# Another order of the steps in the period of the long attentions

## The chip, the cores and the metric

The kernel runs on one core of one Trainium2 chip. The metric is the time of one execution on the device, in microseconds (us); less is better. The engines are TensorE (PE; its weight loads are PEld), VectorE (DVE), ScalarE (ACT), GpSimd (POOL) and SyncE (SP), each with its own in-order program, tied by semaphores.

## The reference, cut to what matters

```python
# L0, L2 and L3 each hold one attention of 448 tokens (8 batches x 56) over a context of 1500 positions per batch
q = heads(norm(x) @ Wq + bq)                    # 16 heads of 8 features
k, v = heads(norm(context) @ Wkv + bkv)         # L0 modulates norm(context); L3 uses the context as it is
attn = softmax(q @ k.T / sqrt(8))
x = x + (attn @ v) @ Wp + bp
```

Between them stand a single-head attention over the same context and three experts (L1), self-attentions over the 56 tokens, and MLPs. The change touches the three long attentions alone.

## The kernel before

A `Heads` object emits one long attention. Its unit is a **period**: the work around the scores of one batch n. TensorE, ScalarE, VectorE and GpSimd each have a list of step names (`self.orders`, built in `Heads.__init__`), and `run` emits them in that order. A step works for batch n, n+1 or n+2 (its lead), so that a period holds:

- for n: `S0`..`S11`, the scores of a chunk of 125 keys each (8 products into one of two score buffers, line 568); on ScalarE `E0`..`E11`, their exponential (line 660); `PV0`..`PV5`, probabilities times values of two chunks (24 products, line 580). `S` of chunk c waits for `E` of c-2, `PVk` for `E(2k+1)`.
- for n-1: `OT`, `OTT`, turning and normalising its output (lines 598 to 609; VectorE lines 706 to 725).
- for n+1: `M0.0`..`M2.7`, 24 products of 128x500 scores each (line 554), of which VectorE takes the maximum (line 687); then VectorE's `maxall`, `maxb`, `part0`, `part1` (lines 690 to 699), TensorE's `MTa`, `MTb` (line 544), which turn the maxima, and `shift0` (VectorE, line 703) and `shift1` (ScalarE, line 664), which copy them into two rows of the queries. `S0` of the next period waits for both.
- for n+2: `T0`..`T2`, transposes of the normalised context (line 523, only where `hat` is set, the first two attentions; ScalarE line 624), `K0`..`K2`, key projections (line 531; each read by two copies on ScalarE, `k0.j` and `Kj`, line 642; GpSimd then splits the rest and SP's DMAs stack the parts, line 365), and `V0`..`V2`, value projections (line 538; two copies on ScalarE, lines 648 and 649).

`T`, `K`, `V`, `M`, `MT`, `OT` and `OTT` write one of three PSUM banks of a ring, `ring_ps`. `ring_banks` hands them out in TensorE's order (the bank of `K1` and `K2` is passed over for a while), and a step waits until the reader of the bank's last user is done. VectorE's list follows TensorE's. ScalarE's is written out in the old kernel: `V0`, `V1`, `shift1`, `V2` come after `E11`.

The old order on TensorE with T steps, with its banks:

```
S0 M0.0:0 M0.1:1 S1 OT:2 T0:0 T1:1 T2:2 M0.2:0 S2 OTT:1 PV0 K0:2 S3 M0.3:0 M0.4:1 S4 K1:2 M0.5:0 PV1 M0.6:1
S5 M0.7:0 M1.0:1 M1.1:2 S6 M1.2:0 PV2 M1.3:1 S7 K2:2 M1.4:0 M1.5:1 S8 M1.6:0 M1.7:1 PV3 M2.0:2 S9 M2.1:0 M2.2:1
S10 M2.3:2 M2.4:0 PV4 M2.5:1 S11 M2.6:2 M2.7:0 V0:1 PV5 V1:2 MTa:0 MTb:1 V2:2
```

`later_periods` runs a fill (maxima of batch 0, its own list `fill`), a period for batch 0, four periods (batches 1 to 4) in a loop with register addresses, and batches 5, 6 and 7 straight; in batch 6's period nothing is left to do for n+2, in batch 7's nothing for n+1.

Of the kernel before, what the change touches and what calls it, by code (L numbers as in the profile page):

```python
# [25 lines left out]
NPV = NC // 2  # L26
# [179 lines left out]
def pixart_program(nc, ctx_nat, ctx_T, x_T, cond_T, weights, vectors, identity, out):  # L206
    ctx = ExitStack()
    with ctx:
# [6 lines left out]
        def sem(name):  # L215
            return ctx.enter_context(nc.semaphore(name))
# [158 lines left out]
        class Heads:  # L375
            def __init__(self, tag, wkey, wval, bkey, bval, hat, modulated=False):
                self.tag, self.wkey, self.wval, self.bkey, self.bval = tag, wkey, wval, bkey, bval
                self.hat, self.modulated = hat, modulated
                J = range(NJ)
                mm = [f"M{j}.{p}" for j in J for p in range(PAIRS)]  # L380
                self.mm = mm
                T3 = [f"T{j}" for j in J] if hat else []

                if hat:
                    beside = {0: mm[0:2], 1: ["OT", *T3, mm[2]], 2: ["OTT", "K0"], 3: mm[3:5], 4: ["K1", *mm[5:7]],
                              5: mm[7:10], 6: mm[10:12], 7: ["K2", *mm[12:14]], 8: mm[14:17], 9: mm[17:19],
                              10: mm[19:22], 11: mm[22:24]}
                else:
                    beside = {0: mm[0:1], 1: ["K0", "OT", mm[1]], 2: ["OTT", mm[2]], 3: ["K1", *mm[3:5]], 4: mm[5:7],
                              5: ["K2", *mm[7:9]], 6: mm[9:12], 7: mm[12:14], 8: mm[14:17], 9: mm[17:19],  # L390
                              10: mm[19:22], 11: mm[22:24]}
                pe = []
                for c in range(NC):

                    more = beside.get(c, [])
                    pe += [f"S{c}", *more[:-1]] + ([f"PV{c // 2 - 1}"] if c and c % 2 == 0 else []) + more[-1:]
                pe += ["V0", f"PV{NPV - 1}", "V1", "MTa", "MTb", "V2"]

                act = []
                for c in range(NC):  # L400
                    act += [f"E{c}", *(T3 if c == 1 else [])]
                    for j in J:
                        if f"K{j}" in beside.get(c, []):
                            act += [f"k0.{j}", f"K{j}"]
                act += ["V0", "V1", "shift1", "V2"]
                read = {"OT": ["sum0", "sum1", "norm0", "norm1"], "OTT": ["OTT"], **{m: [m] for m in mm}}
                dve = ["O", *[r for n in pe for r in read.get(n, [])], "maxall", "maxb", "part0", "part1", "shift0"]
                pool = (["deps", "dpow", "norm", "hat0", "hat1", "hat2"] if hat else []) + [f"{s}{j}" for j in J for s in ("rest", "k1.", "k2.")]
                LEAD = {"S": 0, "P": 0, "E": 0, "O": -1, "s": -1, "n": -1, "T": 2, "K": 2, "V": 2, "k": 2, "h": 2, "r": 2, "d": 2}

                def lead(n):
                    return 2 if n == "norm" else 1 if n in ("shift0", "shift1") else LEAD.get(n[0], 1)

                self.lead = lead
                if modulated:
                    fill = [*mm[0:8], "T0", *mm[8:10], "T1", *mm[10:12], "T2", "K0", *mm[12:16], "K1", *mm[16:20], "K2",
                            *mm[20:24], "V0", "V1", "MTa", "MTb", "V2"]
                else:
                    fill = [*T3, "K0", "K1", "K2", "V0", "V1", *mm, "MTa", "MTb", "V2"]
                self.fill = fill  # L420
                self.orders = {"pe": pe, "act": act, "dve": dve, "pool": pool}

                of_context = {"pe": "TKV", "act": "TkKV", "dve": (), "pool": "dnhrk"}

                def context(eng, n):
                    mine = of_context[eng]
                    return n in mine if isinstance(mine, tuple) else n[0] in mine

                self.context = context
                self.plans = {}  # L430
                for eng, order in self.orders.items():
                    for which in (False, True):
                        steps = [(n, lead(n)) for n in order if context(eng, n) == which]
                        kind = "context" if which else "attention"
                        self.plans[eng, which] = Periods(sem(f"{tag}_{eng}_{kind}_done"), steps) if steps else None
                self.loaded = [sem(f"{tag}_contextT_loaded{u}") for u in range(2)] if not hat else None
                self.nat_loaded = [sem(f"{tag}_context_loaded{u}") for u in range(2)] if hat else None
                self.stacked = [[sem(f"{tag}_keys_stacked{u}_columns{j}") for j in J] for u in range(2)]
                self.qstacked = sem(f"{tag}_queries_stacked")
                self.rows_clear = sem(f"{tag}_rows_clear")  # L440

                self.reader = {}
                for j in J:
                    self.reader |= {f"T{j}": ("act", f"T{j}"), f"K{j}": ("act", f"K{j}"), f"V{j}": ("act", f"V{j}")}
                for m in mm:
                    self.reader[m] = ("dve", m)
                self.reader |= {"MTa": ("dve", "shift0"), "MTb": ("act", "shift1"), "OT": ("dve", "norm1"),
                                "OTT": ("dve", "OTT")}
# [1391 lines left out]
```

How the kernel before makes its waits and increments, by code:

```python
def wait_steps(eng, n, *steps):  # L171
    last = {}
    for plan, name, d in steps:
        last[plan] = max(last.get(plan, -9999), plan.place(name, d))
    for plan, at in last.items():
        eng.wait_ge(plan.sem, n * len(plan.names) + at)
# [336 lines left out]
                def emit(name, batch, prev, cur, nxt):  # L514
# [3 lines left out]
                    if name[0] == "T":  # L518
                        wait_steps(pe, n, self.at("pool", f"hat{name[1:]}"), *free)
                        j = int(name[1:])
                        for c in range(CJ):
                            last = pe.transpose(ps[:, c * CK:(c + 1) * CK], hat_sb[:, j * CJ + c, :],
                                                ident[0:CK, 0:CK])
                    elif name[0] == "K":
                        j = int(name[1:])
                        if self.loaded and j == 0:
                            pe.wait_ge(self.loaded[u], 16 * (half + 1))
                        wait_steps(pe, n, *([self.at("act", f"T{j}")] if self.hat else []), *free)
                        last = pe.matmul(ps[:, 0:KB], self.wkey, self.context_T(u)[:, j * KB:(j + 1) * KB],
# [15 lines left out]
                        j, p = (int(t) for t in name[1:].split("."))  # L547
                        if p == 0:
                            pe.wait_ge(self.stacked[u][j], REPLICA * (half + 1))
                        if name == self.mm[0]:
                            pe.wait_ge(self.qstacked, REPLICA)
                            pe.wait_ge(self.rows_clear, 1)
```

## Time and profile before

| | us |
|---|---|
| median of 3 runs | 1091.48 (1089.87 to 1096.06) |
| profiled execution | 1089.86 |
| its span | 1088.0 |
| TensorE busy | 956.8 (88%) |
| VectorE busy | 583.2 (54%) |
| ScalarE busy | 516.7 (47%) |
| GpSimd busy | 364.6 (34%) |

The long attentions take some 225 us each: about 45 to 285 us, 510 to 733 and 845 to 1058 of the span. Busy time of TensorE is modelled from the start of a product to the end of its result, so it says less than the distance from one step's start to the next. A bracket behind a row of the timeline is idle time of that engine just before it and what ended it.

### The profile page before, as it was taken

Reading aid. Unit: us, or ns where it says so; the run is one execution under the profiler, and the core shown is the slowest. Engines: PE = TensorE matmul, PEld = TensorE weight load, DVE = VectorE, ACT = ScalarE, POOL = GpSimd, SP = SyncE. Lnnn points to the kernel's source line nnn. Section 1 sums busy time; section 2 is a strip of 40 time slices with the busy share of each in tenths; the row PEclk is TensorE's granted clock in tenths of the full one; section 3 lists DMA queues with packets and bytes.
Section 4 is the critical chain, followed back from the end, with each engine's and each line's share of the span. In section 5 each row is a group of like instructions: output and inputs, shape, how many; then the busy total and the mean of one; then the engine's idle time right before and its main releaser. Section 6 shows DMA issues by size and latency. Waiting matters only on the chain.

```text
span 1088.0 us, 25068 instructions
## 1 busy us (share of the span) xinstructions
PE 956.8 (88%) x9448; PEld 619.3 (57%) x9448; DVE 583.2 (54%) x1281; ACT 516.7 (47%) x766; POOL 364.6 (34%) x489
## 2 busy tenths in 40 slices
PE   5659999998889988897899999978798899999977
PEld 3436666666556644583466666653385466666653
DVE  7575666666122166213666666735412666666735
ACT  5636666665223222313366666551222266666541
POOL 6565555540000003315555556110301333333100
PEclk9679999999989999658799999999867699999999
DMA  9753443437025311404344443200230644443200
GB/s 249 174 142 89 111 111 105 109 91 244 1 86 169 98 44 43 135 24 120 97 111 114 110 113 90 69 33 26 77 87 21 172 116 115 120 122 100 58 2 9
DMA packets 76823, 106.25 MB, mean 98 GB/s; under 512 B 9370, under 2 KB 70426, under 8 KB 76480
## 3 DMA queue, kind: packets, MB, share of 16 engines
q1 hardware_dynamic: 75152, 102.26, 34.0%
q10 hardware_dynamic: 1584, 2.79, 0.9%
q8 instruction: 60, 0.98, 0.4%
q14 instruction: 27, 0.22, 0.1%
HBM read 41.17 MB, written 0.23 MB: 38 GB/s over the span
## 4 chain that ended last, share of the span: by engine, by line
PE 64%; DVE 15%; issue 10%; ACT 6%; POOL 2%; DMA 1%; SPq 0%; ACTq 0%; POOLq 0%; DVEq 0%
PE oacc_ps L580 10%; PE ring_ps L554 10%; PE score_ps L568 7%; DVE max_sb L687 7%; PE ring_ps L538 6%; PE ring_ps L531 6%; PE oacc_ps L896 4%; PE ring_ps L1165 3%; PE oacc_ps L335 3%; PE ring_ps L1043 2%; PE score_ps L1035 2%; PE ring_ps L544 2%; PE ring_ps L523 2%; ACT key_sb L642 1%; PE ring_ps L1026 1%
## 5 line engine op out<-in xcount | busy, mean ns | idle before, releaser
L687 DVE TENSOR_REDUCE max_sb<-ring_ps 128x1 f32<-128x500 f32 x576 | 356.4, 673 | 174.2 <-PE ring_ps L554 174.1
L660 ACT ACTIVATE prob_sb<-score_ps 125x896 f32<-125x896 f32 x288 | 257.3, 919 | 132.5 <-PE score_ps L568 131.8
L554 PE MATMUL ring_ps<-kstack,qstack 128*128 128x500 bf16 x576 | 203.8, 392 | 25.0 <-DVE max_sb L687 17.1
L765 POOL TENSOR_TENSOR key_sb<-key_sb,part_sb 128x500 f32<-128x500 f32 x72 | 82.0, 1139 | 280.1 <-ACT key_sb L642 280.1
L568 PEld LDWEIGHTS score_ps<-qstack,kstack 128*128 128x128 bf16 (+1 forms) x2304 | 145.4, 102 | 48.4 <-issue 7.6
L568 PE MATMUL score_ps<-qstack,kstack 128*128 128x112 bf16 (+3 forms) x2304 | 167.4, 214 | 2.4 <-ACT qstack L664 2.3
L580 PE MATMUL oacc_ps<-prob_sb,val_sb 125*32 125x168 f32 (+1 forms) x3456 | 139.5, 294 | 12.7 <-ACT prob_sb L660 12.3
L580 PEld LDWEIGHTS oacc_ps<-prob_sb,val_sb 125*32 125x32 f32 x3456 | 97.7, 109 | 51.7 <-ACT prob_sb L660 23.6
L554 PEld LDWEIGHTS ring_ps<-kstack,qstack 128*128 128x128 bf16 (+1 forms) x576 | 52.5, 98 | 111.2 <-issue 59.7
L335 PE MATMUL oacc_ps<-ident,mean_mat 128*128 128x512 bf16 x326 | 90.3, 417 | 0.0
L756 POOL TENSOR_SCALAR hat_sb<-nat_sb,norm_now 125x128 f32<-125x128 f32 x192 | 87.7, 480 | 4.9 <-POOL norm_now L746 4.9
L772 POOL TENSOR_TENSOR part_sb<-key_sb,part_sb 128x500 bf16<-128x500 f32 x72 | 81.7, 1135 | 5.8
L1209 POOL TENSOR_TENSOR tok_rstd<-tok_var,minus_half 112x4 f32<-112x4 f32 x8 | 8.1, 1010 | 211.5 <-DVE tok_var L1223 211.5
L531 PE MATMUL ring_ps<-ctxT_sb,w_sb 128*128 128x500 f32 x96 | 58.8, 701 | 11.2 <-ACT key_sb L642 8.5
L642 ACT ACTIVATE part_sb<-ring_ps,vec_sb 128x500 bf16<-128x500 f32 x72 | 49.1, 682 | 33.5 <-PE ring_ps L531 31.0
L648 ACT COPY val_sb<-ring_ps 125x384 f32<-125x384 f32 x72 | 34.6, 481 | 56.2 <-PE ring_ps L538 56.2
L335 PEld LDWEIGHTS oacc_ps<-ident,mean_mat 128*128 128x128 bf16 x326 | 33.1, 107 | 44.5 <-issue 21.9
L538 PE MATMUL ring_ps<-w_sb,ctxT_sb 128*125 128x128 f32 x384 | 55.7, 292 | 1.8 <-ACT val_sb L649 1.5
L1243 ACT COPY qpart_sb<-prob_sb 64x448 bf16<-64x448 bf16 x30 | 16.9, 562 | 83.1 <-DVE prob_sb L1232 82.3
L1165 PE MATMUL ring_ps<-tok,w_sb 128*128 128x448 f32 x102 | 46.3, 587 | 10.2 <-DVE part_sb L1797 3.6
L538 PEld LDWEIGHTS ring_ps<-w_sb,ctxT_sb 128*125 128x125 f32 x384 | 47.9, 196 | 11.8 <-DVE max_sb L687 4.6
L523 PE MATMUL ring_ps<-ident,hat_sb 125*128 125x125 f32 x192 | 29.0, 300 | 23.8 <-DVE max_sb L687 9.0
(207 smaller groups left out, 1084.6 us busy)
## 6 DMA issues: line engine op xcount, KB each, us to landing
kstack<-part_sb SPq DMA_DIRECT2D x432, 125.0 KB, 2.4
nat_sb<-ctx_nat SPq DMA_DIRECT2D x24, 672.0 KB
nat_sb<-ctx_T SPq DMA_DIRECT2D x8, 750.0 KB, 4.3
qstack<-qpart_sb SPq DMA_DIRECT2D x24, 224.0 KB, 3.6
w_sb<-ctx_nat SPq DMA_DIRECT2D x5, 672.0 KB
w_sb<-weights SPq DMA_DIRECT2D x1, 3076.5 KB, 12.4
ctxT_sb<-ctx_T SPq DMA_DIRECT2D x4, 750.0 KB, 6.3
part_sb<-ctx_T SPq DMA_DIRECT2D x4, 750.0 KB, 5.9
```

The costliest lines, as they stand in the source:

```text
L335: pe.matmul(out.rearrange("p (a k) -> p a k", a=2), busy_lhs, busy_rhs, start=True, stop=True)
L531: last = pe.matmul(ps[:, 0:KB], self.wkey, self.context_T(u)[:, j * KB:(j + 1) * KB], start=True, stop=True)
L538: last = pe.matmul(ps[0:CK, c * D:(c + 1) * D], self.context_T(u)[:, k0:k0 + CK], self.wval, start=True, stop=True)
L554: last = pe.matmul(ps[:, 0:KB], queries(p, n, D), kstack[:, u, p, j * KB:(j + 1) * KB], start=True, stop=True)
L568: last = pe.matmul(score_ps[0:window(c), c % 2, p // 4, at:at + 2 * LQ], kstack[:, u, p, c * CK:c * CK + window(c)], queries(p, n), start= ...
L580: return pe.matmul(oacc_ps[tile * GW:(tile + 1) * GW, at:at + nh * LQ], val_sb[0:CK, u, c, g * GW:(g + 1) * GW], prob_sb[0:CK, c % PROBS, ...
L660: ins = act.activation(dst, score_ps[0:CK, c % 2, :, 0:HALF], ACT.Exp)
L687: ins = dve.tensor_reduce(max_sb[:, p, j:j + 1], ring_ps[:, self.bank[name], 0:KB], AX.X, ALU.max)
L756: ins = pool.tensor_scalar(hat_sb[:, c, :], nat_sb[0:CK, u, c, :], norm_now[:, 1, c:c + 1], norm_now[:, 0, c:c + 1], ALU.add, ALU.mult)
L765: ins = pool.tensor_tensor(rest, rest, part_sb[:, 0, cols], ALU.subtract)
L772: ins = pool.tensor_tensor(part_sb[:, 2, cols], rest, part_sb[:, 1, cols], ALU.subtract)
L1165: last = pe.matmul(self.ps(name) if out is None else out, lhsT, rhs, start=(k == 0), stop=(k == len(pairs) - 1))
```

## The change

TensorE's list is written out in slots: steps ahead of a chunk's scores, the scores, steps beside them. Two M steps now come ahead of `S0`; the others stand one or two at a time between the rest; `V0` and `V1` stand among the scores (ahead of `S9` and behind `S10` with T steps, ahead of `S8` and `S10` without); `T0`, `T1`, `T2` are apart from each other; `V2` comes ahead of `MTa`. `PVk` comes right behind `S(2k+2)`, and one M stands between `S11` and `PV5` instead of two and `V0`. ScalarE's list is drawn from TensorE's, so its copies of T, K and V stand among the exponentials where their products do. The fill lists put `V2` ahead of `MTa`.

```diff
                 if hat:
-                    beside = {0: mm[0:2], 1: ["OT", *T3, mm[2]], 2: ["OTT", "K0"], 3: mm[3:5], 4: ["K1", *mm[5:7]],
-                              5: mm[7:10], 6: mm[10:12], 7: ["K2", *mm[12:14]], 8: mm[14:17], 9: mm[17:19],
-                              10: mm[19:22], 11: mm[22:24]}
+                    slots = [([], "S0", mm[2:4]), (["OT", mm[4], "T0"], "S1", [mm[5]]), (["OTT", "T1"], "S2", ["PV0", mm[6]]),
+                             (["T2", mm[7]], "S3", [mm[8]]), (["K0"], "S4", ["PV1", *mm[9:11]]), ([mm[11]], "S5", ["K1", mm[12]]),
+                             ([], "S6", ["PV2", *mm[13:15]]), (["K2"], "S7", mm[15:17]), ([], "S8", ["PV3", *mm[17:19]]),
+                             (["V0"], "S9", mm[19:21]), ([], "S10", ["PV4", "V1", *mm[21:23]]), ([], "S11", [mm[23]])]
                 else:
-                    beside = {0: mm[0:1], 1: ["K0", "OT", mm[1]], 2: ["OTT", mm[2]], 3: ["K1", *mm[3:5]], 4: mm[5:7],
-                              5: ["K2", *mm[7:9]], 6: mm[9:12], 7: mm[12:14], 8: mm[14:17], 9: mm[17:19],
-                              10: mm[19:22], 11: mm[22:24]}
-                pe = []
-                for c in range(NC):
-
-                    more = beside.get(c, [])
-                    pe += [f"S{c}", *more[:-1]] + ([f"PV{c // 2 - 1}"] if c and c % 2 == 0 else []) + more[-1:]
-                pe += ["V0", f"PV{NPV - 1}", "V1", "MTa", "MTb", "V2"]
-
-                act = []
-                for c in range(NC):
-                    act += [f"E{c}", *(T3 if c == 1 else [])]
-                    for j in J:
-                        if f"K{j}" in beside.get(c, []):
-                            act += [f"k0.{j}", f"K{j}"]
-                act += ["V0", "V1", "shift1", "V2"]
+                    slots = [([], "S0", mm[2:4]), (["OT", mm[4]], "S1", [mm[5]]), (["OTT", "K0"], "S2", ["PV0", mm[6]]),
+                             ([mm[7]], "S3", [mm[8]]), (["K1"], "S4", ["PV1", *mm[9:11]]), ([mm[11]], "S5", [mm[12]]),
+                             (["K2"], "S6", ["PV2", mm[13]]), ([mm[14]], "S7", mm[15:17]), (["V0"], "S8", ["PV3", *mm[17:19]]),
+                             ([mm[19]], "S9", [mm[20]]), (["V1"], "S10", ["PV4", mm[21]]), ([mm[22]], "S11", [mm[23]])]
+                pe = [*mm[0:2]]
+                for ahead, scores, beside in slots:
+                    pe += [*ahead, scores, *beside]
+                pe += [f"PV{NPV - 1}", "V2", "MTa", "MTb"]
...
+                at_act = {"T": lambda n: [n], "K": lambda n: [f"k0.{n[1:]}", n], "S": lambda n: [f"E{n[1:]}"], "V": lambda n: [n]}
+                act = [step for n in pe if n[0] in at_act for step in at_act[n[0]](n)] + ["shift1"]
```

The new orders, with the banks that `ring_banks` gives:

```
with T:    M0.0:0 M0.1:1 S0 M0.2:2 M0.3:0 OT:1 M0.4:2 T0:0 S1 M0.5:1 OTT:2 T1:0 S2 PV0 M0.6:1 T2:2 M0.7:0 S3 M1.0:1
           K0:2 S4 PV1 M1.1:0 M1.2:1 M1.3:2 S5 K1:0 M1.4:1 S6 PV2 M1.5:2 M1.6:1 K2:2 S7 M1.7:0 M2.0:1 S8 PV3 M2.1:0
           M2.2:1 V0:2 S9 M2.3:0 M2.4:1 S10 PV4 V1:2 M2.5:0 M2.6:1 S11 M2.7:2 PV5 V2:0 MTa:1 MTb:2
without T: M0.0:0 M0.1:1 S0 M0.2:2 M0.3:0 OT:1 M0.4:2 S1 M0.5:0 OTT:1 K0:2 S2 PV0 M0.6:0 M0.7:1 S3 M1.0:2 K1:0 S4
           PV1 M1.1:1 M1.2:2 M1.3:1 S5 M1.4:2 K2:0 S6 PV2 M1.5:1 M1.6:2 S7 M1.7:1 M2.0:2 V0:0 S8 PV3 M2.1:1 M2.2:2
           M2.3:0 S9 M2.4:1 V1:2 S10 PV4 M2.5:0 M2.6:1 S11 M2.7:2 PV5 V2:0 MTa:1 MTb:2
ScalarE, with T: E0 T0 E1 T1 E2 T2 E3 k0.0 K0 E4 E5 k0.1 K1 E6 k0.2 K2 E7 E8 V0 E9 E10 V1 E11 V2 shift1
```

## Rows read from the trace of the kernel before

**Rows 1.** The page: busy time by engine, and the chain that ended last.
```profile
PE 956.8 (88%) x9448; PEld 619.3 (57%) x9448; DVE 583.2 (54%) x1281; ACT 516.7 (47%) x766; POOL 364.6 (34%) x489
...
PE 64%; DVE 15%; issue 10%; ACT 6%; POOL 2%; DMA 1%; SPq 0%; ACTq 0%; POOLq 0%; DVEq 0%
```

**Rows 2.** Windows cut at `part0`: stretch, length, busy us (instructions), clock, DMA.
```profile
104.73:216.93 112.20, 106.89 (x1304) 72.47 (x1294) 70.41 (x140) 74.72 (x114) 65.93 (x98) 1.00 0.41 111
216.93:243.40 26.47, 25.64 (x322) 17.35 (x318) 17.56 (x36) 18.26 (x28) 13.40 (x19) 1.00 0.33 88
243.40:265.90 22.50, 21.00 (x312) 14.34 (x301) 17.07 (x36) 12.59 (x19) 0.00 (x0) 1.00 0.94 304
555.08:665.70 110.62, 106.56 (x1304) 72.30 (x1293) 70.39 (x141) 72.94 (x114) 65.91 (x98) 1.00 0.42 113
...
887.46:992.28 104.82, 100.34 (x1248) 66.96 (x1242) 69.23 (x140) 67.05 (x102) 34.59 (x36) 1.00 0.42 118
992.28:1017.34 25.06, 24.32 (x318) 16.30 (x312) 17.15 (x36) 16.39 (x27) 8.65 (x9) 1.00 0.35 94
```

**Rows 3.** Timeline of TensorE, straight-line period: start, length, step.
```profile
218.00 1.04 PE L544 MATMUL ring_ps<-ident,maxparts 128*2 128x128 f32 x8
218.90 1.14 PE L538 MATMUL ring_ps<-w_sb,ctxT_sb 128*125 128x128 f32 x8
219.91 0.55 PE L568 MATMUL score_ps<-qstack,kstack 128*128 128x112 bf16 x8
...
226.24 0.56 PE L568 MATMUL score_ps<-qstack,kstack 128*128 128x112 bf16 x8
226.63 0.58 PE L554 MATMUL ring_ps<-kstack,qstack 128*128 128x500 bf16 x2
227.06 0.56 PE L568 MATMUL score_ps<-qstack,kstack 128*128 128x112 bf16 x8
...
242.82 0.97 PE L580 MATMUL oacc_ps<-prob_sb,val_sb 125*32 125x168 f32 x24
243.72 1.14 PE L538 MATMUL ring_ps<-w_sb,ctxT_sb 128*125 128x128 f32 x8
```

**Rows 4.** Timeline, end of the period without context steps (batch 6).
```profile
263.31 0.62 PE L568 MATMUL score_ps<-qstack,kstack 128*125 128x112 bf16 x8
...
263.97 0.92 ACT L660 ACTIVATE prob_sb<-score_ps 125x896 f32<-125x896 f32 x1 [1.30 <-PE score_ps L568]
264.94 0.73 PEld L580 LDWEIGHTS oacc_ps<-prob_sb,val_sb 125*32 125x32 f32 x24 [1.07 <-ACT prob_sb L660]
264.94 0.97 PE L580 MATMUL oacc_ps<-prob_sb,val_sb 125*32 125x168 f32 x24 [0.58 <-ACT prob_sb L660]
...
268.01 0.95 PE L568 MATMUL score_ps<-qstack,kstack 128*128 128x112 bf16 x16 [0.78 <-ACT qstack L664]
```

**Rows 5.** Timeline around `K2` of a loop period.
```profile
207.07 1.06 PE L531 MATMUL ring_ps<-ctxT_sb,w_sb 128*128 128x500 f32 x2
...
207.97 0.58 PE L554 MATMUL ring_ps<-kstack,qstack 128*128 128x500 bf16 x2
...
208.18 0.68 ACT L642 ACTIVATE part_sb<-ring_ps,vec_sb 128x500 bf16<-128x500 f32 x1
...
209.31 0.92 ACT L660 ACTIVATE prob_sb<-score_ps 125x896 f32<-125x896 f32 x1
```

**Rows 6.** Timeline of VectorE and ScalarE: eight maxima in a row, `V0`'s first copy.
```profile
238.04 4.91 DVE L687 TENSOR_REDUCE max_sb<-ring_ps 128x1 f32<-128x500 f32 x8 [0.52 <-PE ring_ps L554]
...
242.93 0.48 ACT L648 COPY val_sb<-ring_ps 125x384 f32<-125x384 f32 x1 [0.54 <-PE ring_ps L538]
```

**Rows 7.** Timeline of TensorE: `S0` of a loop period.
```profile
192.07 1.02 PE L568 MATMUL score_ps<-qstack,kstack 128*128 x8
```

**Rows 8.** Windows, columns as in Rows 2: end of stage two's fill, batch 7's period.
```profile
524.00:531.00 7.00, 5.07 (x18) 2.52 (x18) 4.75 (x12) 0.52 (x1) 3.41 (x8) 0.50 0.26 86
266.00:285.00 19.00, 13.98 (x260) 10.53 (x261) 2.44 (x10) 10.88 (x13) 0.00 (x0) 1.00 0.02 5
```

More of the change, by code:

```diff
@@ new lines, in __init__ @@
+                pe = [*mm[0:2]]
+                for ahead, scores, beside in slots:
+                    pe += [*ahead, scores, *beside]
+                pe += [f"PV{NPV - 1}", "V2", "MTa", "MTb"]
+                assert sorted(n for n in pe if n[0] == "M" and n[1] != "T") == sorted(mm)
+                at_act = {"T": lambda n: [n], "K": lambda n: [f"k0.{n[1:]}", n], "S": lambda n: [f"E{n[1:]}"], "V": lambda n: [n]}
+                act = [step for n in pe if n[0] in at_act for step in at_act[n[0]](n)] + ["shift1"]
@@ L416, in __init__ @@
                     fill = [*mm[0:8], "T0", *mm[8:10], "T1", *mm[10:12], "T2", "K0", *mm[12:16], "K1", *mm[16:20], "K2",
-                            *mm[20:24], "V0", "V1", "MTa", "MTb", "V2"]
+                            *mm[20:24], "V0", "V1", "V2", "MTa", "MTb"]
                 else:
-                    fill = [*T3, "K0", "K1", "K2", "V0", "V1", *mm, "MTa", "MTb", "V2"]
+                    fill = [*T3, "K0", "K1", "K2", "V0", "V1", *mm, "V2", "MTa", "MTb"]
                 self.fill = fill
```

## The prediction, made before the changed kernel was run

> **What bounds the kernel now.** I read the page first: TensorE is busy 88% of the span and 64% of the chain that ended last, VectorE 15%, ScalarE 6% [rows 1]. So TensorE's program order sets the time, and a step put elsewhere costs what TensorE then waits. Next the stage windows: a steady period of a long attention (one batch) takes 112.20 / 4 = 28.05 us in the first stage, 110.62 / 4 = 27.66 in the second, 104.82 / 4 = 26.21 in the third (no T steps); those are the four periods in the program's loop. The straight-line period behind them takes 26.47 and 25.06 us, and the one that has no context steps left 22.50 [rows 2]. The clock is at its upper level in all. The timeline then gives the price of each step, and what can be late.
>
> **Unit prices**, as the distance to the next step on TensorE: S 0.39 us, M (43 / 2) 0.21, PV 0.90, V 1.0, MTa and MTb together 0.90 [rows 3], K 0.90 [rows 5] (its reader starts 1.11 after it starts, so a result is seen about 0.2 after its stream ends). T (0.44), OT (0.78) and OTT (0.25) I take from the same stretch; they don't change. Sum of a period with T steps: 12 x 0.39 + 24 x 0.21 + 6 x 0.90 + 3 x 1.0 + 3 x 0.92 + 3 x 0.44 + 0.90 + 0.78 + 0.25 = about 24.2 us; without T 22.9. The straight-line periods leave 26.47 - 24.2 = 2.2 us of waits, and 25.06 - 22.9 = 2.1. Placing the old order step by step with these prices (a step starts when its engine is free and its releaser is done) gives 26.1 and 25.0 us, with waits of 1.9 and 2.1, nearly all of them M steps waiting for a ring bank whose maximum VectorE has not read; so I trust the method to about 0.4 us a period. VectorE starts a maximum each (4.91 - 0.68) / 7 = 0.60 us [rows 6], TensorE can issue one in 0.21; between stretches of maxima VectorE idles.
>
> **The change, part by part.** No instruction is added or removed: the 24.2 us of TensorE work stand, and so do the work of ScalarE and VectorE. Only waits change. I place the new order in the same way.
>
> (a) M steps spread out, two ahead of S0. This removes the old bank waits at M1.0, M1.6, M1.7, M2.4 and V0 (about 1.4 us in my placement). But with three banks, new neighbours meet: K2 now takes the bank of M1.5 with only M1.6 between. M1.5 starts, VectorE 0.41 later, its maximum takes 0.68: K2 can start at 1.14, TensorE arrives at 0.42, a wait of 0.72. OT waits for the maximum of M0.1 (0.39), T0 for M0.3 (0.22), OTT (0.20), K0 (0.21, behind T2's copy), K1 (0.11), small ones 0.1. Sum 1.95. In the stage without T: M1.3 0.72, M1.7 0.33, M2.0 0.39, V1 0.39, OT 0.39, K0 0.40, OTT 0.21, two of 0.11: 3.05.
>
> (b) PV5 follows S11 with one M between. The nearest row is the period without context steps: S11 starts at 263.31, its exponential at 263.97, PV5 at 264.94, which is 1.63 after S11, with 0.58 us idle although two M stand between [rows 4]. In a full period before, V0 fills this gap. After the change S11 (0.45) and one M (0.21) fill 0.66 of 1.6: a wait of 0.93 in every period. I take 0.93; the ends are 0.58 (the row) and 1.0.
>
> (c) ScalarE's order. Its list now follows TensorE's, so the two copies of K2 (0.57 each, 1.13 from the first copy to the exponential behind [rows 5]) stand right ahead of E7, and V0's two copies (the first takes 0.48 [rows 6]; both, queued, I estimate at 0.64) ahead of E9. E7 starts 0.2 + 1.15 after K2's stream ends, which is when S7 starts, and ends at 2.27; TensorE has S7, two M and S8 (1.21) and then stands at PV3, which needs E7: a wait of 1.1. In the same way PV4 waits for E9: 0.2 + 0.63 + 0.92 against 1.21, that is 0.54 to 0.6. Before, K2's copies came behind E7 and two more exponentials' worth of TensorE work lay ahead of PV3; V0 and V1 came after the last exponential. Behind PV3 on TensorE stand M2.1, M2.2, V0 and all that follows, so VectorE starves too. In the stage without T, K2 stands ahead of S6 and V0 ahead of S8, with no odd E right behind, and neither wait appears. Below, each could be zero if TensorE came late enough anyway; I keep that for the range.
>
> (d) V2 moves ahead of MTa. Before, V2 (1.0 us) ran while the two shift rows were copied into the queries; S0 followed at once (218.00, 218.90, 219.91 [rows 3]). Where no V2 stands there, S0 stands idle for 0.78 us [rows 4]. Now M0.0 and M0.1 (0.42) stand there, M0.1 itself in the bank of MTa and so behind its copy: 0.35 to 0.5 us of waiting per period. In exchange V2 covers the chain from the last maximum to the maxparts, but that chain was covered before by V0, PV5 and V1: no gain in a full period. S0 behind these two M asks for nothing else new: the keys' columns that M0.0 reads were stacked a period ago (DMA issues lie near the middle of a period), so SP's queue adds nothing; its waits on S3, S7, S11 keep their place. POOL works 65.93 / 4 = 16.5 us of 28 [rows 2] and has slack of over 1 us at T0.
>
> Sums of a straight-line period: with T 1.95 + 0.93 + 1.1 + 0.57 + 0.35 = 4.9 us of waits for 1.9, **+3.0**; without T 3.05 + 0.93 + 0.4 = 4.4 for 2.1, **+2.3 to +2.8**. The period without context steps: +1.4 and +1.2 (PV waits and the bank waits of paired M). The first straight-line period like a full one, +2.7 and +2.5; the last, scores and PV only, +0.5 to +1.4.
>
> (e) The loop. There S0's eight products take 1.02 instead of 0.55 us [rows 3, 7], each held up before it issues, and the loop period is 1.6 us longer than the straight one. With waits at the head of the period a part of this is hidden. My placement gives 29.8 with T and 28.2 without, so +1.75 (28.05) and +2.1 (27.66) and +2.0 (26.21); if the old loop's whole excess stays, +2.5, +2.5, +2.3.
>
> Stage one: 2.7 + 4 x 1.75 to 2.5 + 3.0 + 1.4 + 1.0 = 15.1 to 18.1. Stage two: 8.1 + 4 x 2.1 to 2.5 = 16.5 to 18.1. Stage three: 2.5 + 4 x 2.0 to 2.3 + 2.7 + 1.2 + 1.0 = 15.4 to 16.6. In the fill of stages two and three V2 now runs in a wait of about 2 us before MTa: -2 each. In all 47.0 + 0 to 52.8 less 4: **43 to 49 us**; I take 47. The profiled execution had 1089.86 us for a span of 1088.0, the median of the runs is 1091.48; on 1090 that gives **1137 us**.
>
> **TensorE's clock.** More waiting could lower it. In the last period of an attention TensorE is busy 13.98 of 19.00 us and granted the full 2.4 GHz; ahead of stage two's start, with 5.07 of 7.00, it is at 1.2 GHz, inherited from a slow fill [rows 8]. A period after the change is busy 24.2 of 29, more than the first of these. The Trainium skill, TensorE: Matmul & The Clock Gate, section What's actually happening, says that the throttled state is the default and activity releases it; by that rule too, waits of about 1 us spread over a period matter little. The same page (Architectural detail: the array is 16x 32x32) lets the queue pull weight loads ahead of products in flight. If it did so across a wait, a PV wait would cost some 0.1 us less; in the row for PV5 the load stands idle as well, 1.07 us [rows 4], so the sum keeps the whole wait.
>
> **Rivals.**
> - Faster. ScalarE is idle a third of the period and VectorE 40%; if copies and exponentials keep up, so that the waits of (c) and K2's bank wait don't appear, what remains is 0.93 + 0.35 + about 0.6 = 1.9 us, against 2.2, and in the loop half a us more is hidden. That is 18 x 0.3 + 12 x 0.8 = 15 us less: **1075**. It decides at PV3: it holds if E7 ends by 1.2 us after S7 starts, where I have 2.27. For it: the spread of VectorE's work is real. Against it: strict order on ScalarE, and the measured PV5 wait, which nothing here removes.
> - No change, **1090**: the gains of (a) equal (b) and (d), and (c) is about half its size.
> - Clock: if waits at the head and at PV3 let the clock drop to 1.2 GHz for a fifth of each period, 5 us more each over some 18 periods: **1225**.
> - The order doesn't reach the chip as written: not likely, since each engine's list is emitted from it; the waits follow the same names.
>
> **Chances.** The forecast, slower with 1108 to 1152, 0.81; clock 0.03; faster 0.11; no change 0.05. So slower by over 0.5% 0.84, within 0.5% (about what a measurement can tell from none) 0.05, faster 0.11. The range leaves out the faster rival, the clock and no change: 1108 is my sum with the waits of (c) halved and the loop's excess fully hidden; 1152 has them all with 0.1 us more latency on each exponential.
>
> **What would show it.** In the changed profile: a full period of about 29.5 (with T) and 28 (without) us; the waits list with PV behind the exponential at well over the present count, some 3 a period with T and 1 without; K2 idle behind a maximum by 0.7; S0 idle behind the shift copy by 0.1 to 0.3; VectorE's idle time spread out; S0 in the loop still slow. I am wrong if PV3 follows S8 at once.

## The result and the profile after

The changed kernel takes **1131.0 us** (1130.1 to 1135.5), the kernel before 1091.4 us (1089.9 to 1096.1), medians of four runs each on one chip: 1.0365 times the time before, interval 1.0329 to 1.0401. The profiled execution has a span of 1128.1 us against 1088.0.

The page of the changed kernel first, which answers to [rows 1]:

```profile
PE 961.5 (85%) x9448; PEld 620.3 (55%) x9448; DVE 581.1 (52%) x1281; ACT 517.6 (46%) x766; POOL 364.5 (32%) x489
...
PE 60%; DVE 15%; issue 11%; ACT 10%; POOL 2%; DMA 1%; SPq 0%; ACTq 0%; DVEq 0%; POOLq 0%
```

No engine has more to do: instruction counts are the same and the busy times stand within 5 us. The only share of the chain that grew by more than a point is ScalarE's, 6% to 10%, and TensorE's fell from 64% to 60%. So more of the chain runs through ScalarE; the waits below say where.

The windows, cut at the cast of `maxparts` as in [rows 2] (stretch, length, busy us of TensorE, its loads, VectorE, ScalarE, GpSimd, then clock, DMA share, GB/s):

```profile
107.22:228.64 121.42, 108.38 (x1300) 73.09 (x1292) 70.08 (x140) 74.19 (x112) 65.86 (x97) 1.00 0.37 103
228.64:258.28 29.64, 26.23 (x328) 17.81 (x322) 17.36 (x36) 18.55 (x28) 11.44 (x15) 1.00 0.29 79
258.28:282.04 23.76, 20.54 (x296) 13.48 (x292) 16.90 (x36) 12.18 (x15) 0.00 (x0) 1.00 0.88 293
569.68:689.00 119.32, 107.91 (x1300) 72.98 (x1292) 70.01 (x140) 72.21 (x112) 65.89 (x97) 1.00 0.39 104
...
915.61:1028.32 112.71, 102.88 (x1248) 67.52 (x1244) 67.46 (x140) 66.73 (x100) 34.48 (x36) 1.00 0.39 110
1028.32:1055.99 27.67, 25.00 (x318) 16.36 (x314) 16.85 (x35) 16.69 (x25) 8.62 (x9) 1.00 0.31 85
```

Divide the loop windows by four: 30.36, 29.83 and 28.18 us a period, where [rows 2] give 28.05, 27.66 and 26.21. The straight period behind them went from 26.47 to 29.64 and from 25.06 to 27.67, and the one without context steps from 22.50 to 23.76. The clock is 1.00 in every window.

The waits list (engine, line, what it waited for: us in total, times, longest), first of the changed kernel:

```profile
PEld oacc_ps L576 <- ACT prob_sb L656: 56.6, 64, 1.2
PE oacc_ps L576 <- ACT prob_sb L656: 43.3, 63, 1.1
PE ring_ps L550 <- DVE max_sb L683: 25.4, 50, 9.0
PE ring_ps L527 <- DVE max_sb L683: 8.8, 18, 0.7
```

then of the kernel before:

```profile
PE oacc_ps L580 <- ACT prob_sb L660: 12.3, 18, 1.1
```

L576 after is L580 before: PV behind an exponential. It went from 18 waits to 63 and from 12.3 to 43.3 us. Some 10.6 us of either figure stand in the last periods (five waits in each of the three), which the change left as they were.

Now TensorE in the straight period of the first stage, with ScalarE's rows between K2 and PV3 (start, length, step; a bracket is idle time ahead of the row and its releaser). It answers to [rows 3, 4, 5]:

```profile
245.30 0.60 PE L550 MATMUL ring_ps<-kstack,qstack 128*128 128x500 bf16 x2
246.54 1.08 PE L527 MATMUL ring_ps<-ctxT_sb,w_sb 128*128 128x500 f32 x2 [0.65 <-DVE max_sb L683]
247.46 0.56 PE L564 MATMUL score_ps<-qstack,kstack 128*128 128x112 bf16 x8
247.66 0.68 ACT L638 ACTIVATE part_sb<-ring_ps,vec_sb 128x500 bf16<-128x500 f32 x1 [1.71 <-PE ring_ps L527]
248.27 0.56 PE L564 MATMUL score_ps<-qstack,kstack 128*128 128x112 bf16 x8
248.79 1.73 ACT L656 ACTIVATE prob_sb<-score_ps 125x896 f32<-125x896 f32 x2
249.76 0.97 PE L576 MATMUL oacc_ps<-prob_sb,val_sb 125*32 125x168 f32 x24 [0.94 <-ACT prob_sb L656]
...
252.79 0.56 PE L564 MATMUL score_ps<-qstack,kstack 128*128 128x112 bf16 x8
253.69 0.97 PE L576 MATMUL oacc_ps<-prob_sb,val_sb 125*32 125x168 f32 x24 [0.35 <-ACT prob_sb L656]
...
255.99 0.62 PE L564 MATMUL score_ps<-qstack,kstack 128*125 128x112 bf16 x8
256.47 0.39 PE L550 MATMUL ring_ps<-kstack,qstack 128*128 128x500 bf16 x1
...
257.61 0.97 PE L576 MATMUL oacc_ps<-prob_sb,val_sb 125*32 125x168 f32 x24 [0.76 <-ACT prob_sb L656]
258.51 1.14 PE L534 MATMUL ring_ps<-w_sb,ctxT_sb 128*125 128x128 f32 x8
259.49 1.04 PE L540 MATMUL ring_ps<-ident,maxparts 128*2 128x128 f32 x8
260.48 0.70 PE L550 MATMUL ring_ps<-kstack,qstack 128*128 128x500 bf16 x2
261.30 0.55 PE L564 MATMUL score_ps<-qstack,kstack 128*128 128x112 bf16 x8
```

Read it downwards. K2 (246.54) starts 1.24 us after M1.5 (245.30), held by a maximum. K2's copy on ScalarE starts at 247.66 and keeps E7 and E8 (248.79, two exponentials in 1.73 us) back, and PV3 stands idle 0.94 us, until 249.76. PV4 stands 0.35 and PV5 0.76 us. At the head S0 starts 1.81 us after the shift rows' first product (259.49). A bracket counts from the modelled end of the product before, so in these rows it is some 0.17 us shorter than what the prediction works with, the distance from start to start less the unit prices. By that measure K2 waits 1.24 - 0.42 = 0.82 us, PV3 (249.76 after 248.27) 1.49 - 0.39 = 1.10, PV4 (253.69 after 252.79) 0.51, and PV5 (257.61 after 256.47) 1.14 - 0.21 = 0.93.

### The profile page after: what moved, and what is told of

It reads as the page before. It is cut to its first block, busy times and chain, and to the rows that moved or that the text cites. A ratio compares the mean times of both kernels' runs of the same rounds, so it can differ in the third digit from the quotient of the medians.

```text
span 1128.1 us, 25030 instructions
## 1 busy us (share of the span) xinstructions
PE 961.5 (85%) x9448; PEld 620.3 (55%) x9448; DVE 581.1 (52%) x1281; ACT 517.6 (46%) x766; POOL 364.5 (32%) x489
## 4 chain that ended last, share of the span: by engine, by line
PE 60%; DVE 15%; issue 11%; ACT 10%; POOL 2%; DMA 1%; SPq 0%; ACTq 0%; DVEq 0%; POOLq 0%
PE oacc_ps L576 11%; PE ring_ps L550 8%; PE score_ps L564 7%; PE ring_ps L534 7%; DVE max_sb L683 6%; PE ring_ps L527 6%; ACT prob_sb L656 4%; PE oacc_ps L892 4%; PE ring_ps L1161 3%; PE ring_ps L519 2%; PE oacc_ps L335 2%; PE ring_ps L1039 2%; PE score_ps L1031 2%; PE ring_ps L540 1%; PE ring_ps L1022 1%
## 5 line engine op out<-in xcount | busy, mean ns | idle before, releaser
L656 ACT ACTIVATE prob_sb<-score_ps 125x896 f32<-125x896 f32 x288 | 260.3, 920 | 93.8 <-PE score_ps L564 93.4
L550 PE MATMUL ring_ps<-kstack,qstack 128*128 128x500 bf16 x576 | 198.8, 395 | 32.1 <-DVE max_sb L683 25.4
L576 PE MATMUL oacc_ps<-prob_sb,val_sb 125*32 125x168 f32 (+1 forms) x3456 | 139.5, 294 | 43.4 <-ACT prob_sb L656 43.3
L576 PEld LDWEIGHTS oacc_ps<-prob_sb,val_sb 125*32 125x32 f32 x3456 | 97.6, 109 | 71.2 <-ACT prob_sb L656 56.6
L550 PEld LDWEIGHTS ring_ps<-kstack,qstack 128*128 128x128 bf16 (+1 forms) x576 | 48.7, 98 | 105.7 <-issue 56.0
L335 PE MATMUL oacc_ps<-ident,mean_mat 128*128 128x512 bf16 x326 | 87.5, 406 | 0.0
L534 PEld LDWEIGHTS ring_ps<-w_sb,ctxT_sb 128*125 128x125 f32 x384 | 49.6, 199 | 12.3 <-ACT key_sb L638 3.4
L335 PEld LDWEIGHTS oacc_ps<-ident,mean_mat 128*128 128x128 bf16 x326 | 32.5, 105 | 43.1 <-issue 19.4
L519 PE MATMUL ring_ps<-ident,hat_sb 125*128 125x125 f32 x192 | 34.0, 307 | 17.8 <-ACT ctxT_sb L620 6.3
```

Source lines behind the costliest of these rows:

```text
L335: pe.matmul(out.rearrange("p (a k) -> p a k", a=2), busy_lhs, busy_rhs, start=True, stop=True)
L534: last = pe.matmul(ps[0:CK, c * D:(c + 1) * D], self.context_T(u)[:, k0:k0 + CK], self.wval, start=True, stop=True)
L550: last = pe.matmul(ps[:, 0:KB], queries(p, n, D), kstack[:, u, p, j * KB:(j + 1) * KB], start=True, stop=True)
L576: return pe.matmul(oacc_ps[tile * GW:(tile + 1) * GW, at:at + nh * LQ], val_sb[0:CK, u, c, g * GW:(g + 1) * GW], prob_sb[0:CK, c % PROBS, ...
L656: ins = act.activation(dst, score_ps[0:CK, c % 2, :, 0:HALF], ACT.Exp)
```

## The experiments

Ratios are to the kernel before, timed on the same chip (1091.8 us beside e1 to e4, 1091.5 beside e5 to e8, 1091.0 beside e9 to e12); the interval is in brackets.

### The parts of the change, one at a time

**e1: V0, V1 and V2 back at their old places**, on TensorE, on ScalarE and in the fills; the rest as changed.

```diff
-                             (["V0"], "S9", mm[19:21]), ([], "S10", ["PV4", "V1", *mm[21:23]]), ([], "S11", [mm[23]])]
+                             ([], "S9", mm[19:21]), ([], "S10", ["PV4", *mm[21:23]]), ([], "S11", [mm[23]])]
...
-                pe += [f"PV{NPV - 1}", "V2", "MTa", "MTb"]
+                pe += ["V0", f"PV{NPV - 1}", "V1", "MTa", "MTb", "V2"]
...
```

> The kernel after the change, but V0, V1 and V2 back where they stood before (V0 ahead of PV5, V1 behind it, V2 behind MTb, on TensorE, on ScalarE and in the fill); the new places of M, T and K stay. Theory 1 (each wait as placed step by step: PV5 0.93 us, PV4 0.5, the head of a period 0.4): about 1.5 us less per full period with T and 1.3 less without, 26 us less in all, 1105 us. PV5 no longer idle; PV3 still idle by about 1.1 behind the exponential. Theory 2 (the spread M steps and their bank waits are the whole loss): no change, 1131. Theory 3 (the value projections are the whole loss): 1091.

1112.3 us, 1.0186 [1.0157, 1.0216]: 18.7 us of the 40 come back, where 26 were expected. PV waits for the exponential 39 times (26.9 us) instead of 63, so V0 in PV5's gap does its work; the loop period is 28.92 instead of 30.36 us.

**e2: E7 ahead of K2's copies and E9 ahead of V0's** in ScalarE's list, with T steps.

```diff
+                if hat:
+                    for name, ahead_of in (("E7", "k0.2"), ("E9", "V0")):
+                        act.remove(name)
+                        act.insert(act.index(ahead_of), name)
```

> The kernel after the change, with one thing different: in ScalarE's list, where T steps exist, E7 stands ahead of K2's two copies, and E9 ahead of V0's. Theory 1 (ScalarE's order makes PV3 and PV4 wait): PV3's idle time falls from 0.94 to about 0.3, PV4's to 0.3; 1.0 us less per full period of stages one and two, none in stage three; 12 us less in all, 1119 us. Theory 2 (PV3 would wait anyway, for another releaser): within 2 us of 1131.

1123.6 us, 1.0308 [1.026, 1.0357], runs from 1118.6 to 1131.0. The four runs scatter, and by the intervals alone the gain over the changed kernel (7 us by the medians) isn't clear of noise. The traces settle it: the loop period is 0.9 us shorter in the first and in the second stage, and in the third, where the edit does nothing, it stays at 28.2. The waits of PV fall from 43.3 to 32.5 us; PV3 and PV4 stand idle 0.19 us each instead of 0.94 and 0.35. Over the 12 full periods with T steps ScalarE's order is worth some 11 us.

**e3: K2 ahead of M1.5** instead of behind M1.6, with T steps.

```diff
-                             ([], "S6", ["PV2", *mm[13:15]]), (["K2"], "S7", mm[15:17]), ([], "S8", ["PV3", *mm[17:19]]),
+                             ([], "S6", ["PV2", "K2", *mm[13:15]]), ([], "S7", mm[15:17]), ([], "S8", ["PV3", *mm[17:19]]),
```

> The kernel after the change, with K2 ahead of M1.5 instead of behind M1.6, where T steps exist. Theory 1: K2's wait for the maximum of M1.5 (0.65 us measured) goes, and E7 starts earlier by the 0.4 us of two M steps, so PV3 waits less: 0.8 to 0.9 us less per full period of stages one and two, 10 us less in all, 1121 us. Theory 2 (PV3's wait takes over what K2's gives back): within 2 us of 1131.

1122.9 us, 1.0276 [1.0248, 1.0303]: 8 us for K2's bank wait and what it drags behind it, where 10 were expected. The waits of PV fall to 51 times, 32.1 us: the earlier copies let E7 out in time. M steps wait more instead, 75 times and 30.1 us rather than 50 times and 25.4.

**e4: M0.0 and M0.1 ahead of S0 in the kernel before**, alone.

```diff
+                pe = [*mm[0:2], *[n for n in pe if n not in mm[0:2]]]
```

> The kernel before the change, with M0.0 and M0.1 put ahead of S0 and nothing else. Theory 1 (placed step by step, V2 still covers the shift copies): within 1 us of 1091 in either direction, since no wait stands at S0 for the two to fill. Theory 2 (they fill the slow issue of S0 in the loop, half a us in 12 loop periods): 1085. Theory 3 (they are the harmful part of the change): 1100 or more.

1089.8 us (ten runs), 0.998 [0.9964, 0.9996]: a gain of 0.2%, below what one would act on. In the trace the loop periods are 0.2 to 0.4 us shorter, the straight ones the same within 0.1.

**e6: V2 ahead of MTa in the kernel before**, alone, on both engines and in the fills.

```diff
-                pe += ["V0", f"PV{NPV - 1}", "V1", "MTa", "MTb", "V2"]
+                pe += ["V0", f"PV{NPV - 1}", "V1", "V2", "MTa", "MTb"]
...
-                act += ["V0", "V1", "shift1", "V2"]
+                act += ["V0", "V1", "V2", "shift1"]
...
```

> The kernel before the change, with V2 ahead of MTa and MTb (and ScalarE's copies of V2 ahead of shift1, and V2 ahead of MTa in the fills), nothing else. Theory 1 (V2 covered the copies of the shift rows): S0 stands idle by 0.7 to 0.8 in each of 18 full periods, 13 us more, less about 3 in the fills: 1101 us. Theory 2 (V2 covers as much in front as it did behind): 1088 to 1091.

1103.0 us, 1.0094 [1.0067, 1.012]: V2's place costs 11.4 us by itself when nothing stands ahead of S0. S0 waits for ScalarE's shift copy 24 times, 19.9 us, where it waited 3 times, 2.3 us.

**e5: e1 and e3 together, and E7 ahead of K2's copies**, the last two with T steps only. No edit in it is new.

> The kernel after the change with three things put right at once: V0, V1, V2 where they stood before, K2 ahead of M1.5, and E7 ahead of K2's copies (the last two where T steps exist). Theory 1 (the waits are separate and add up): the first alone took 19 us off, the second 8, the third and its like about 8; they overlap at PV3, so some 5 to 9 us less than with the first alone, 1103 to 1107 us, still above 1091 because of the bank waits of the spread M steps and PV right behind S. Theory 2 (nothing else is left once these are gone): 1091 or less.

1106.9 us, 1.0137 [1.0108, 1.0165]: 15.4 us over the kernel before are left. Its waits of PV for the exponential are 15.7 us, only 3.4 more than before the change. So most of what is left isn't a wait for ScalarE. The places of M, T, K and PV still differ from the kernel before; no run here parts them.

**e8: V1 between M2.7 and PV5**, to fill PV5's gap, in the changed kernel.

```diff
-                             (["V0"], "S9", mm[19:21]), ([], "S10", ["PV4", "V1", *mm[21:23]]), ([], "S11", [mm[23]])]
+                             (["V0"], "S9", mm[19:21]), ([], "S10", ["PV4", *mm[21:23]]), ([], "S11", [mm[23], "V1"])]
...
```

> The kernel after the change, with V1 moved from beside S10 to between M2.7 and PV5, in both kinds of attention. Theory 1 (PV5 waits for E11 because too little stands between them): PV5's idle time (0.76 us) goes, PV4 waits no longer or shorter, 0.9 us less per full period, 16 us less in all, 1115 us. Theory 2 (the wait moves on to V2's bank or to the maxima's chain): 1125 or more.

1115.9 us, 1.0212 [1.0185, 1.0238]: 15 us, as expected. One step of 1.0 us in PV5's gap is worth 0.7 to 0.8 us in each of the 18 full periods.

### The place of the PV steps

**e12: PV0 to PV4 each one chunk later**, behind S3, S5, ... S11 instead of S2, S4, ... S10; nothing else of the changed kernel is touched.

```diff
+                for k in range(NPV - 1):
+                    pe.remove(f"PV{k}")
+                    pe.insert(pe.index(f"S{2 * k + 3}") + 1, f"PV{k}")
```

> The kernel after the change with PV0 to PV4 each one chunk later (behind S3, S5, S7, S9, S11 instead of S2 to S10), nothing else. Theory 1: the waits at PV3, PV4 and PV5 all go, since a score and more stand between an exponential and its reader; bank waits stay (K2, M1.3 and the like); 1.4 us less per full period with T, 2.0 less without, 28 us less in all, 1103 us. Theory 2 (S(c+2) or the fourth probability buffer then waits instead): 1120 or more, with ScalarE's exponential late behind PV.

**1092.4 us** (ten runs), 1.0016 [1.0007, 1.0025]. The changed kernel becomes 38.6 us faster, 10 us more than expected, and as fast as the kernel before. That is not the same as undoing the change. Against the kernel before, its stretches from a stage's first to last cast are 10.6 and 7.3 us longer in the first two stages and 1.3 shorter in the third; the fills and the last periods, 16.7 us shorter in all, make up for it. The last periods alone gain 3.0 us each, and those the change had slowed by 0.11.

TensorE in a full period of the third stage, where no PV but PV5 had waited, shows why. From S6 to S8, first in the changed kernel:

```profile
1043.48 0.56 PE L564 MATMUL score_ps<-qstack,kstack 128*128 128x112 bf16 x8
1043.97 0.97 PE L576 MATMUL oacc_ps<-prob_sb,val_sb 125*32 125x168 f32 x24
1044.87 0.60 PE L550 MATMUL ring_ps<-kstack,qstack 128*128 128x500 bf16 x2
1045.30 0.56 PE L564 MATMUL score_ps<-qstack,kstack 128*128 128x112 bf16 x8
1046.02 0.39 PE L550 MATMUL ring_ps<-kstack,qstack 128*128 128x500 bf16 x1 [0.17 <-DVE max_sb L683]
1046.70 0.37 PE L550 MATMUL ring_ps<-kstack,qstack 128*128 128x500 bf16 x1 [0.29 <-DVE max_sb L683]
1046.91 1.03 PE L534 MATMUL ring_ps<-w_sb,nat_sb 128*125 128x128 f32 x8
1047.78 0.56 PE L564 MATMUL score_ps<-qstack,kstack 128*128 128x112 bf16 x8
```

then with PV one chunk later, and its PV4 behind S11:

```profile
1009.29 0.56 PE L567 MATMUL score_ps<-qstack,kstack 128*128 128x112 bf16 x8
1009.68 0.58 PE L553 MATMUL ring_ps<-kstack,qstack 128*128 128x500 bf16 x2
1010.11 0.55 PE L567 MATMUL score_ps<-qstack,kstack 128*128 128x112 bf16 x8
1010.59 0.97 PE L579 MATMUL oacc_ps<-prob_sb,val_sb 125*32 125x168 f32 x24
1011.49 0.59 PE L553 MATMUL ring_ps<-kstack,qstack 128*128 128x500 bf16 x2
1011.92 1.04 PE L537 MATMUL ring_ps<-w_sb,nat_sb 128*125 128x128 f32 x8
1012.80 0.56 PE L567 MATMUL score_ps<-qstack,kstack 128*128 128x112 bf16 x8
...
1017.22 0.61 PE L567 MATMUL score_ps<-qstack,kstack 128*125 128x112 bf16 x8
1017.77 0.97 PE L579 MATMUL oacc_ps<-prob_sb,val_sb 125*32 125x168 f32 x24
```

S6 to S8 takes 4.30 us in the first and 3.51 us in the second, with the same eight steps. PV2 stood ahead of four maxima with only S7 among them, so VectorE, at 0.60 us each, fell behind; moved behind S7 it stands in the middle of the four and VectorE catches up beside it. And PV4 (1017.77) now fills PV5's gap behind S11. So in this stage the PV steps did two things: they no longer wait for their exponentials, and they are the longest stretch of TensorE work that needs no ring bank. In the first stage the second effect is absent: the waits of M for a bank grow there, from 0.4 us in the four loop periods to 5.4, while those of PV fall from 8.2 us to none.

Period by period (casts of `maxparts`) the 40.1 us between the spans of the changed kernel and of e12 are: 7.8 from the first stage's first to last cast, 7.2 in the second, 15.4 in the third, and 3.4, 3.3 and 3.1 from each stage's last cast to the next fill's, or to the end.

### An order that beats both

**e7: an order placed anew by the unit prices** of the prediction: M mostly singly, PV2 behind S7, PV3 behind S9 and PV4 behind S11 (S10 without T) with further steps between, K2's copies behind E8, V0 and V1 behind S11 (round M2.7 with T steps), V2 last.

```diff
+                    pe = ("M0.0 S0 M0.1 T0 M0.2 S1 M0.3 S2 M0.4 OT M0.5 T1 S3 M0.6 S4 M0.7 OTT PV0 M1.0 T2 K0 M1.1 PV1 S5 "
+                          "M1.2 M1.3 K1 M1.4 S6 M1.5 S7 M1.6 PV2 M1.7 S8 M2.0 M2.1 S9 K2 M2.2 M2.3 PV3 M2.4 S10 M2.5 M2.6 "
+                          "S11 V0 M2.7 V1 PV4 PV5 MTa MTb V2 ").split()
+                    act = ("E0 T0 E1 E2 T1 E3 T2 k0.0 K0 E4 E5 k0.1 K1 E6 E7 E8 k0.2 K2 E9 E10 E11 V0 V1 shift1 V2 ").split()
...
+                    pe = ("M0.0 M0.1 S0 S1 M0.2 K0 M0.3 OT S2 S3 M0.4 M0.5 K1 M0.6 S4 M0.7 S5 OTT PV0 M1.0 M1.1 PV1 M1.2 "
+                          "S6 M1.3 M1.4 S7 M1.5 PV2 M1.6 S8 M1.7 M2.0 S9 K2 M2.1 M2.2 PV3 S10 M2.3 M2.4 M2.5 PV4 M2.6 M2.7 "
+                          "S11 V0 V1 PV5 MTa MTb V2 ").split()
+                    act = ("E0 E1 k0.0 K0 E2 E3 k0.1 K1 E4 E5 E6 E7 E8 k0.2 K2 E9 E10 E11 V0 V1 shift1 V2 ").split()
```

> Both lists written out anew, found by placing steps with the durations of the trace so that no wait is left in a steady period: two or one M ahead of S0, M steps singly, no PV sooner than one or two steps of other work after the exponential it needs, S11 followed by V0 and V1 and two PV before MTa, V2 behind MTb with T steps and ahead of nothing that waits. Theory 1 (TensorE's waits are the only loss above its 24.2 and 22.9 us of work): 24.8 to 25.3 us a full period with T and 23.3 to 23.9 without, 35 us less than before the change, 1057 us. Theory 2 (another limit holds, such as GpSimd's splitting, the key stacking or issue): above 1080, with a wait for one of these in the list.

**1030.5 us**, 0.9434 [0.9409, 0.9458]: 61 us under the kernel before, 26 more than expected. Its windows, columns as above:

```profile
97.94:197.70 99.76, 99.68 (x1296) 71.65 (x1292) 70.94 (x140) 74.06 (x113) 65.34 (x97) 1.00 0.45 125
197.70:222.29 24.59, 24.58 (x338) 17.75 (x334) 17.89 (x35) 18.82 (x30) 16.68 (x24) 1.00 0.37 99
...
931.44:954.42 22.98, 22.98 (x313) 16.09 (x312) 17.33 (x35) 16.36 (x26) 8.58 (x9) 1.00 0.38 103
```

TensorE is busy in all of it, 99.68 of 99.76 us, and a straight period takes 24.59 and 22.98 us where the sum of unit prices was 24.2 and 22.9. The waits list has hardly any PV left:

```profile
PE ring_ps L542 <- DVE max_sb L675: 14.0, 25, 6.2
...
PE oacc_ps L568 <- ACT prob_sb L648: 2.5, 4, 1.1
```

The prices held: from the second one on full periods take 24.3 to 25.0 us with T steps and 23.0 to 23.8 without, about the expected ranges. The expected total did not follow from them. Of the 63.4 us between the two spans 46.0 lie between the first and last casts of the stages, more than the whole 35 that I had put down, and the other 17.4 in the fills and last periods. The loop's excess over the straight period is 0.35 us (24.94 against 24.59) where it was 1.58.

Three kernels take one property of this order away each; their edits are to e7.

**e9: PV2 to PV4 right behind S6, S8 and S10**, as in the change.

```diff
+                for k in (2, 3, 4):
+                    pe.remove(f"PV{k}")
+                    pe.insert(pe.index(f"S{2 * k + 2}") + 1, f"PV{k}")
```

> The new order (e7) with PV2, PV3 and PV4 moved back to right behind S6, S8 and S10, where both other kernels have PV; nothing else. Theory 1 (the distance from an exponential to the PV that reads it is what the new order wins by): PV4 idle by 0.5 us with T steps and 1.4 without, M steps bunched behind it idle by up to 0.7; 2.0 us more per full period, 36 us more in all, 1066 us. Theory 2 (the gain of e7 comes from the spread M steps or the loop): 1035 or less.

1080.3 us, 0.9896 [0.988, 0.9911]: 50 us lost, 36 expected. The waits of PV for the exponential go from 2.5 to 22.9 us and those of M for a bank from 14.0 to 27.9; the rest I did not assign.

**e10: each odd M behind the even one before it.**

```diff
+                for m in mm[1::2]:
+                    pe.remove(m)
+                    pe.insert(pe.index(mm[mm.index(m) - 1]) + 1, m)
```

> The new order (e7) with M steps in pairs (each odd one moved right behind the even one before it); nothing else. Theory 1 (single M steps keep TensorE from waiting for a bank): 0.8 us more per full period, 15 us more in all, 1045 us. Theory 2 (VectorE's queue is short enough either way): within 3 us of 1030.

1051.1 us, 0.9619 [0.9602, 0.9637]: 21 us lost, 15 expected.

**e11: the M steps ahead of S0 behind it.**

```diff
+                ahead = pe[:pe.index("S0")]
+                pe = ["S0", *ahead, *pe[len(ahead) + 1:]]
```

> The new order (e7) with the one (with T steps) or two (without) M steps that stand ahead of S0 put right behind it; nothing else. Theory 1 (they stand where S0 waits for the shift copies): 0.25 us more per full period, 4 us more in all, 1035 us. Theory 2 (they also keep the slow issue of the loop's first products off the path): 10 us more or above.

1036.8 us, 0.9513 [0.9491, 0.9535]: 6 us lost, 4 expected.

In an order with hardly a wait left, two ideas of the change are worth something, 21 us (single M steps) and 6 us (M ahead of S0), beside 50 us for the place of the PV steps. That the PV steps alone hid the two in the changed kernel isn't shown: e12 gives them slack there and is no faster than the kernel before.

## Why the prediction was right

The direction, the waits and the lengths of the full periods came out. The total was 40 us where 47 stood, and most of the difference lies outside the full periods; that it still fell near the stated 43 to 49 is in part luck, as (e) shows.

The sizes below are in the prediction's own measure: start to start, less the unit prices. Added as printed, those give 24.1 and 22.8 us for a period rather than 24.2 and 22.9 (K stands at 0.90 in one place and 0.92 in another); nothing hangs on it.

**(a) Ring banks.** K2 waits 0.82 us for 0.72, its start 1.24 us after M1.5's for 1.14; e3 prices the wait and what follows it at 8 us. In the third stage the straight period is 4.9 us over its unit prices: 0.6 at the head, 0.96 ahead of PV5, 0.5 on the way into the other PV steps (below) and 2.9 at ring banks, for 3.05. Not seen was that the last come from where PV stands as much as from where M stands; e12 removes some 1.4 us of them a period in that stage.

**(b) PV5.** 0.93 us for 0.93, with 0.76 in the bracket; e8, which fills the gap, gives 15 us.

**(c) ScalarE's order.** PV3 starts 2.30 us after S7, where E7's end was put at 2.27, and waits 1.10 us for 1.1; PV4 waits 0.51 for 0.54 to 0.6. In the third stage only PV5 waits: four times in four loop periods, 3.2 us. The faster rival needed PV3 within 1.2 us and falls here. The cause was only partly right: e2 puts the exponentials ahead of the copies and takes away 0.9 us of the 1.6 a period, since PV3 and PV4 still stand close behind S8 and S10. The 32.5 us of waits left in e2 are mostly others: PV5 some 14 us, the last periods 10.6.

**(d) The head.** MTa to S0 is 1.81 us, less 0.90 and 0.42 for the steps in it: 0.49 us of waiting, the upper end of 0.35 to 0.5. I put two M ahead of S0 and V2 ahead of MTa into one term. Apart, in the kernel before, V2 costs 11.4 us (e6) and the two M gain 2 (e4).

**(e) The periods.** Predicted and measured:

| | predicted | measured |
|---|---|---|
| straight, with T (stages one and two) | +3.0 | +3.17, +2.97 |
| straight, without T | +2.3 to +2.8 | +2.61 |
| loop, stages one, two, three | +1.75 to 2.5, +2.1 to 2.5, +2.0 to 2.3 | +2.31, +2.17, +1.97 |
| without context steps | +1.4, +1.2 | +1.26, +1.25, +1.34 |
| first | +2.7, +2.7, +2.5 | +4.67, +1.63, +2.22 |
| last | +0.5 to 1.4 each | +0.11 each |

All rows but the last sum to 44.0 to 49.8 predicted and 46.9 measured. **The terms that were mis-sized** lie between the stages: last periods and fills together came to -1 in the sum and to -6.8 measured. The split flatters the forecast, for V2's -4 was booked in the fills, and by its own mechanism (V2 no longer between the cast and S0) it belongs to the first periods. So booked, the forecast is 40.0 to 45.8 up to the last cast and +3 outside, against 46.9 and -6.8: the two misses have opposite signs and partly cancel.

Of the miss outside, about 2.7 us is the last period. It was priced as if its order had changed; but with the M, K and V steps gone, what the two lists leave, scores with `PVk` behind `S(2k+2)`, is the same in both but for OT and OTT (20.73 us before, 20.84 after, from the cast to the start of the last OTT). The rest is in the fills: the first stage's fill ends (its cast) 2.2 us earlier, which the sum did not have, and those of stages two and three 3.3 and 1.7 us earlier counted from the last period's output product. V2 moved alone (e6) changes the two later stretches, counted from the cast of the last period, by +0.9 and -2.1 us, so its place is not what shortens the second stage's fill. What V2 does there shows behind the cast: S0 follows it by 3.66 us before in both stages and by 2.55 and 2.75 after, 1.1 and 0.9 instead of 2, which helps to keep their first periods below my figure. What shortens the fills stays open.

The first period of stage one grew by 4.67. Both kernels stand there once for VectorE (8.43 us before, 9.04 after), but the old one had put S1 in front of that stall and the new one has not. How the 2 us over my figure split I did not measure.

**The range.** Its lower end, with (c) halved (-10 us) and the loop's excess fully hidden (-9) from the 43, comes to some 1114 us, not 1108. The measured 1131 lies inside either.

**The clock.** Mean granted clock of the span 0.914 before and 0.925 after, 1.00 in every window above: periods with 5.5 us of waits (29.64 less the 24.1 of work), with TensorE idle for 0.94 us at most at a time, kept the upper level, and the clock rival falls. By the rule of the Trainium skill that the prediction cites (TensorE: Matmul & The Clock Gate, What's actually happening), the trace agrees. On its other rule, that loads are pulled ahead of products in flight, PV's loads stand idle behind the exponential too, 64 times and 56.6 us, and the first load of PV5 starts with its product, at 257.61: no load crossed such a wait, and the whole wait was the right price.

**No change** needed (c) at half its size; it was at its full size, 1.10 and 0.51 us.

## What to carry to other kernels

In a program whose engines run in written order, set a product behind the end of what makes its operand, and not behind the instruction that feeds it. Here PV could start 1.6 us after the start of its scores (S11 at 255.99, PV5 at 257.61): 0.66 us until the exponential starts [rows 4], 0.92 for the exponential, and on top of it the copies and exponentials queued ahead. One step of slack at five places made this kernel 39 us faster, and taking slack away at three cost the best one 50. A long step that needs no bank also gives the engine that drains the banks time to catch up; in the third stage it did so from the middle of a run of short steps, and not from its head. An edit that mixes several ideas and loses may hold some that gain: price each step's waits first, then place the order anew from those prices.

## What the runs showed that I had not expected

- The loop's excess over a straight period is not a fixed price. S0's eight products, which take 0.55 us in straight code, still take 1.0 in the loop of the changed kernel:

```profile
201.43 1.03 PE L564 MATMUL score_ps<-qstack,kstack 128*128 x8
```

  but the loop period exceeds the straight one by 1.58 us before, 0.72 after and 0.35 in the new order (first stage). Two M steps ahead of S0 hide 0.3 to 0.4 us of it: with them alone added to the kernel before (e4) the excess is 1.22 us, and without the M ahead of S0 the new order (e11) has 0.64 instead of 0.35. What hides the rest I did not try.
- TensorE pays about 0.1 us on the way from S or M to PV: 0.49 us from S2 to PV0 (1036.27 after 1035.78 in the third stage) where S to M takes 0.39. In the kernel before, K behind S takes 0.40 (233.77 after 233.37), and its type is float32 as PV's is, so it isn't the change of type alone.
- In the second stage's fill the clock was 0.50 with TensorE busy 5.07 of 7.00 us [rows 8]; after the change the stretch at the same distance from the cast was granted 0.63, busy 6.66 of 7.00:

```profile
537.00:544.00 7.00, 6.66 (x32) 3.67 (x32) 5.66 (x14) 1.17 (x3) 3.38 (x8) 0.63 0.30 84
```

  The products ahead of S0 there are then faster too: the shift rows take 1.48 us for 1.87.
